# Adaptive-norm two-layer kernel: the first attention stage in another order, with three of its VectorE pieces on GpSimd

## The chip, the core and the metric

The kernel runs on one core of a Trainium2 chip. TensorE (PE) multiplies matrices, VectorE (DVE), ScalarE (ACT) and GpSimd (POOL) work element by element, and SyncE (SP) only issues transfers. Each engine takes its own instructions strictly in the order in which the program lists them; between engines, semaphores hold an instruction until its operands are there. The metric is the time of one execution on the device, in microseconds (us), as the median of the runs.

## What is computed

Two layers, each an attention part and a mixture of experts, each behind a layer norm that a vector `c` modulates. The change touches the attention part of the first layer, for x of 2048 positions by 128 channels:

```python
h = _layernorm(x, axis=-1) * (1 + ca) + sa
z = conv1d(h @ W_in, w_conv, 4 taps, causal, per channel) + b_conv
x_val, x_gate, s_raw = z[..., :D], silu(z[..., D:2*D]), z[..., 2*D:]
time_w = exp(-softplus(slopes) * distance)          # one rate per head, 32 heads
p = exp(clip(score_scale * s_raw, -20.0, 20.0))
phi = x_val * theta                                  # 4 angles per channel
w = softmax(deriv_logits)
poly = w[0] + w[1] * x_val - w[2] * square(x_val)    # the derivative polynomial
p_w = p * time_w                                     # the decayed weights
num_re, num_im, den = cumsum([p_w*poly*cos(phi), p_w*poly*sin(phi), p_w], axis=position)
re, im = num_re / max(den, 1e-4), num_im / max(den, 1e-4)
rsq = rsqrt((sum(re**2) + sum(im**2)) / 32 + 1e-5)   # per head
y = re * rsq * norm_scale @ W_re + im * rsq * norm_scale @ W_im
x = x + ga * (y * x_gate @ W_out)
```

Behind it come the first layer's experts and the whole second layer, which the change leaves as they are.

## The kernel before

**Layout.** Channels lie on the 128 partitions, positions along the free axis, cut into four chunks of 512 (`NC`, `CW`). One instruction over a chunk works on 128x512 elements; one over the four angles of a chunk on 128x2048.

**Start (lines 1651 to 1703).** SP issues the small vectors, both layers' modulation matrices `wmod`, the four pieces of x and the weights. DVE spreads `silu(c)`, PE multiplies it with both `wmod` matrices, DVE turns the results into `modc` and `gar` for both layers, multiplies input and convolution weights into `wfold` (three groups: values, gates, scores), and then does the first layer norm of the four pieces. PE turns each piece (`norm`, line 849), ACT writes it as `hT` (line 1384).

**Projections (line 868).** `values0`, `gates0` and `scores0` of a chunk are four matmuls each, one per tap. PE does values of chunk 0, then the scores of all four chunks, then gates of chunk 0; the others follow inside the loop.

**Weights and angles.** DVE scales and clips a chunk's scores (lines 1814, 1815), ACT takes the exponential (line 1446), and DVE multiplies by the decay table `tw` (line 1819), all four chunks before the loop. `front(c)` on DVE makes the four angles and reduces them to a turn (lines 1719, 1721, 1722); `trig(c)` on ACT takes |x|, cosine and sine (lines 1406 to 1409). `weights(c)` on DVE does the polynomial (1730, 1734), its product with the weights (1735) and the running sum of the denominator (1732).

**The loop over chunks.** `back(c)` on DVE multiplies cosines and sines with the weights (lines 1744, 1745) and makes eight running sums (`TENSOR_TENSOR_SCAN`, line 1752). PE multiplies each sum into `y` as it comes (line 903), ACT squares them (1418), PE adds the squares (909). `mean_square(c)` on DVE floors and squares the denominator (1757, 1758) and adds it (1760), ACT takes the root (1423), `gated(c)` on DVE inverts it (1766), multiplies by the gate and by `y` (1768, 1770), PE multiplies by `W_out` (921), `residual(c)` adds x (1774). DVE's order in round c is `back(c)`, `mean_square(c-1)`, `front(c+1)`, `weights(c+1)`, `gated(c-1)`. PE's in round c is values and gates of chunk c+1, `out0(c-2)`, then the products of chunk c.

**Behind the loop.** The second layer norm (lines 1651 to 1664 again), for which PE first does twenty matmuls with the identity whose result nobody reads (`spare`, line 838), then the router and the experts. GpSimd does almost nothing in this stage.

## Time and profile before

| | us |
|---|---|
| median of 3 runs | 1192.84 |
| lowest and highest | 1191.51, 1195.95 |
| the profiled execution | 1191.35 |
| its span | 1189.6 |
| first attention stage and second norm, in the span | from 0 to about 192 |

The profile holds one execution. DVE is busy for 77% of the span, PE for 91%, ACT for 62%, GpSimd for 21%. A timeline row gives the start and the length in us, the engine, the line, the operation, its output and inputs, the number of instructions and, in brackets, how long the engine sat idle before and which instruction ended that. Rows that hold several instructions give their length together. One matmul of the program on 32-bit numbers is two records of PE, so a projection of four matmuls is eight.

### The profile page before, as it was taken

The numbers are of one execution on the slowest core, as the hardware profiler recorded it, in microseconds if no ns is written. First come the engines' busy times: TensorE is split into PE (matmuls) and PEld (weight loads), VectorE is DVE, ScalarE is ACT, GpSimd is POOL, SyncE is SP. The second block draws the span as 40 slices with busy tenths as digits, with TensorE's granted clock in tenths as the row PEclk, the third lists the DMA queues.
The fourth block names the chain that finished last, engine by engine and source line by source line (L and its number), as shares of the span: only waits on it lengthen the run. The fifth ranks groups of instructions, "written<-read, shape, count | busy, mean of one in ns | idle before, by whom it ended". The sixth has DMA issues, their size and how long they took to land.

```text
span 1189.6 us, 18272 instructions
## 1 busy us (share of the span) xinstructions
PE 1079.5 (91%) x5695; PEld 600.4 (50%) x5711; DVE 916.6 (77%) x1791; ACT 740.3 (62%) x1088; POOL 247.7 (21%) x287
## 2 busy tenths in 40 slices
PE   3898668999999988989999999999979999999998
PEld 2333236477777743322222222222335888888886
DVE  5589998455555485899999999988637888888885
ACT  1645426588888723455667676778765666666664
POOL 0000001289988914431111100111120000000000
PEclk9899879999999999899999999999998999999999
DMA  6000001599898352430000000000000410111001
GB/s 178 1 0 1 1 0 49 110 219 203 195 206 181 71 140 53 66 96 2 2 1 2 2 1 2 1 2 2 1 2 3 160 56 29 40 62 62 0 1 36
DMA packets 40206, 66.58 MB, mean 56 GB/s; under 512 B 14778, under 2 KB 31322, under 8 KB 34778
## 3 DMA queue, kind: packets, MB, share of 16 engines
q1 hardware_dynamic: 40130, 65.56, 22.8%
q8 instruction: 48, 0.79, 0.3%
q14 instruction: 28, 0.23, 0.1%
HBM read 62.30 MB, written 3.11 MB: 55 GB/s over the span
## 4 chain that ended last, share of the span: by engine, by line
PE 61%; DVE 26%; ACT 6%; issue 4%; POOL 1%; DMA 0%; SPq 0%; POOLq 0%; DVEq 0%; ACTq 0%
PE ps L1015 10%; PE ps L1016 10%; PE ps L1017 10%; PE ps L1242 9%; DVE arena_b L2008 8%; PE ps L1178 7%; DVE arena_b L1752 3%; PE ps L1225 3%; PE ps L836 3%; PE ps L1191 2%; POOL parts L775 1%; DVE arena_b L1933 1%; ACT arena_b L1565 1%; PE ps L868 1%; DVE arena_b L2015 1%
## 5 line engine op out<-in xcount | busy, mean ns | idle before, releaser
L1565 ACT ACTIVATE arena_b<-ps 128x1024 f32<-128x1024 f32 (+3 forms) x320 | 272.9, 894 | 134.6 <-PE ps L1225 133.1
L1015 PE MATMUL ps<-parts 128*128 128x512 f32 x640 | 252.5, 394 | 10.2 <-POOL parts L775 7.7
L1017 PE MATMUL ps<-parts 128*128 128x512 f32 x640 | 249.3, 390 | 0.0
L1016 PE MATMUL ps<-parts 128*128 128x512 f32 x640 | 249.3, 390 | 0.0
L2008 DVE TENSOR_REDUCE arena_b<-ps 128x1 f32<-128x512 f32 x384 | 237.9, 682 | 7.0 <-PE ps L1178 5.7
L1178 PE MATMUL ps<-arena_a 48*128 48x512 bf16 (+6 forms) x820 | 180.4, 309 | 17.8 <-DVE arena_b L2008 9.0
L775 POOL TENSOR_TENSOR parts<-arena_b,parts 128x512 fp32r<-128x512 f32 x128 | 166.6, 1313 | 61.4 <-ACT parts L1498 56.8
L1178 PEld LDWEIGHTS ps<-arena_a 48*128 48x128 bf16 (+1 forms) x832 | 60.3, 94 | 204.8 <-DVE arena_b L2008 132.7
L1242 PE MATMUL ps<-arena_b 128*32 128x512 f32 (+3 forms) x1280 | 151.1, 544 | 1.6 <-ACT arena_b L1565 0.8
L1933 DVE SCALAR_TENSOR_TENSOR arena_b<-ps,arena_a 128x512 f32<-128x512 f32 x128 | 87.0, 688 | 79.8 <-PE ps L1017 79.8
L1015 PEld LDWEIGHTS ps<-parts 128*128 128x128 f32 x640 | 120.1, 188 | 48.0 <-POOL parts L775 19.7
L1017 PEld LDWEIGHTS ps<-parts 128*128 128x128 f32 x640 | 120.1, 188 | 25.2
L1016 PEld LDWEIGHTS ps<-parts 128*128 128x128 f32 x640 | 120.2, 188 | 23.7
L1225 PE MATMUL ps<-arena_a 50*128 50x512 bf16 (+3 forms) x640 | 126.4, 351 | 6.0 <-ACT arena_b L1565 4.8
L2115 DVE TENSOR_TENSOR arena_b<-ps,arena_b 128x512 f32<-128x512 f32 x128 | 88.2, 689 | 52.6 <-PE ps L1017 46.8
L1592 ACT ACTIVATE arena_b<-ps 128x512 f32<-128x512 f32 x128 | 76.6, 599 | 82.9 <-PE ps L1017 82.6
L819 POOL TENSOR_SCALAR_AFFINE_SELECT arena_b<-arena_b 128x256 f32<-128x256 f32 x128 | 52.1, 408 | 365.2 <-ACT arena_b L1565 364.1
L1497 ACT ACTIVATE arena_b<-arena_b 128x512 f32<-128x512 f32 x128 | 80.3, 628 | 36.5 <-DVE arena_b L1933 35.4
L2120 DVE TENSOR_TENSOR parts<-arena_b,parts 128x512 fp32r<-128x512 f32 x128 | 87.2, 681 | 0.1
L1596 ACT ACTIVATE parts<-arena_b 128x512 fp32r<-128x512 f32 x128 | 79.8, 624 | 0.4 <-DVE arena_b L2115 0.4
L1498 ACT ACTIVATE parts<-arena_b 128x512 fp32r<-128x512 f32 x128 | 78.9, 616 | 0.0
L2010 DVE TENSOR_REDUCE arena_b<-ps 128x4 f32<-128x512 f32 x64 | 43.0, 690 | 19.5 <-PE ps L1191 19.0
(276 smaller groups left out, 1133.8 us busy)
## 6 DMA issues: line engine op xcount, KB each, us to landing
arena_a<-root_weights SPq DMA_DIRECT2D x60, 512.0 KB, 6.4
arena_b<-expert_weights SPq DMA_DIRECT2D x7, 1024.0 KB, 6.2
arena_a<-q_parts SPq DMA_DIRECT2D x36, 64.0 KB
wslot<-in_L_ffn_up_w SPq DMA_DIRECT2D x8, 256.0 KB, 6.7
wslot<-in_L_ffn_down_w SPq DMA_DIRECT2D x8, 256.0 KB, 7.0
wslot<-in_L_ffn_w_gate SPq DMA_DIRECT2D x8, 256.0 KB, 2.7
wslot<-in_L_ffn_w_up SPq DMA_DIRECT2D x8, 256.0 KB, 3.0
wslot<-in_L_ffn_w_down SPq DMA_DIRECT2D x8, 256.0 KB, 3.6
```

What stands on the lines that cost most here:

```text
L775: g.tensor_tensor(hid0[:, k % NBUF, 1, :], sq0[:, k % NBUF, :], hid0[:, k % NBUF, 0, :].bitcast(F32), ALU.subtract).then_inc(moe_lo, 1)
L1015: mm(bank, w(0), x(0), start=start, stop=False)
L1016: mm(bank, w(0), x(1), start=False, stop=False)
L1017: return mm(bank, w(1), x(0), start=False, stop=stop)
L1178: return mm(b[:, at_:at_ + kw], qst[r, tq // TPC, g, i // 2, tq % TPC * P:(tq % TPC + 1) * P], kst[r, i % 2, g, k0:k0 + kw], start=True, s ...
L1225: last = mm(ps[:, 2 + 2 * pair + i, off:CW], kst[r, i, g, j * P:(j + 1) * P], qst[r, c, g, pair, off:CW], start=True, stop=True)
L1242: last = mm(ps[32 * i:32 * i + 32, 6, off:CW], vaug[:, j, g, :], probs[:, s % 2, i, off:CW], start=(j == 0), stop=(j == TPC * c + TPC - 1) ...
L1565: a(probs[:, s % 2, 2 * pair:2 * pair + 2, off:CW], ps[:, 2 + 2 * pair:4 + 2 * pair, off:CW], ACT.Exp, scale=scale).then_inc(p2_exp, 1)
L1933: v.scalar_tensor_tensor(prod0[:, k % NBUF, :], ps[:, k % 4, :], 0.0, cbw[:, pair % NCBUF, chunk(c)], ALU.max, ALU.mult).then_inc(moe_prod, 1)
L2008: v.tensor_reduce(m8[:, t % TPC, 4 + u:5 + u], b, AX_X, ALU.max).then_inc(slot_read, 1)
L2115: v.tensor_tensor(prod1[:, k % NBUF, :], ps[:, 2 + k % 2, :], silg[:, k % 2, :], ALU.mult)\
L2120: v.tensor_tensor(hid1[:, k % NBUF, 1, :], prod1[:, k % NBUF, :], hid1[:, k % NBUF, 0, :].bitcast(F32), ALU.subtract).then_inc(ffn_lo, 1)
```

## The change

SP: the second layer's `wmod` is loaded behind the convolution weights, and the decay table counts on `ld_b`, so that weights no longer wait for it. PE: only layer 0's modulation comes first; ten spare matmuls; turning, values and scores are interleaved; layer 1's modulation goes to bank 6; six projections instead of three stand ahead of the router's transpose, and `values0` runs two chunks ahead. ACT: `trig(0)` and `trig(1)` both come ahead of the loop, the exponentials of the scores of chunks 1 to 3 inside round 0. DVE: the statistics of x start before the modulation, `front` runs two chunks ahead (its first two ahead of the loop), scores 2 and 3 are scaled between the running sums of chunk 0, layer 1's modulation and two of the four pieces' statistics for the second norm stand ahead of the last `mean_square`, and `weights(c)` is the running sum alone. GpSimd: `polynomial(c)` and `floor(c)`, seven instructions for each chunk. `floor` multiplies by the root of 1e-5 before it squares, where DVE scaled the square. Nothing else of the arithmetic changes.

```diff
             nc.gpsimd.memset(hT[:, 0:PAD], 0.0).then_inc(pad_zero, 1)
...
+            def polynomial(c):
+
+                x, t, part = xv[:, c % 2, :], tmp[:, 0, :], pw[:, chunk(c)]
+                pool.wait_ge(xv_ready, c + 1)
+                if c == 0:
+                    pool.wait_ge(slope_ready, 2)
+                    pool.wait_ge(tw_ready, 1)
+                pool.wait_ge(zs_exp, c + 1)
+                nc.gpsimd.tensor_tensor(part, part, tw[:, chunk(c)], ALU.mult).then_inc(pw_ready, 1)
+                chain(nc.gpsimd.tensor_scalar(t, x, dw[:, 2:3], dw[:, 1:2], ALU.mult, ALU.add))
+                chain(nc.gpsimd.tensor_tensor(t, t, x, ALU.mult))
+                chain(nc.gpsimd.tensor_scalar(t, t, dw[:, 0:1], None, ALU.add))
+                if c >= 2:
+                    pool.wait_ge(num_ready, 2 * M0 * (c - 2) + 1)
+                nc.gpsimd.tensor_tensor(pw_poly[:, c % 2, :], t, part, ALU.mult).then_inc(pw_ready, 1)
+
+            def floor(c):
+
+                t = tmp[:, 1 + c % 2, :]
+                pool.wait_ge(xv_used, c + 1)
+                if c >= 2:
+                    pool.wait_ge(q_ready, c - 1)
+                chain(nc.gpsimd.tensor_scalar(t, den[:, chunk(c)], 1e-4, EPS ** 0.5, ALU.max, ALU.mult))
+                nc.gpsimd.tensor_tensor(t, t, t, ALU.mult).then_inc(pw_ready, 1)
+
+            for c in range(NC):
+                polynomial(c)
+                floor(c)
...
             for c in range(NC):
                 if c == 1:
+                    pe.wait_ge(rw_ready, 2)
+                if c + 1 < NC:
+                    gates0(c + 1)
+                if c + 2 < NC:
+                    values0(c + 2)
+                if c == 0:
+                    scores0(3)
                     pe.wait_ge(rw_ready, 1)
...
+            trig(0)
+            trig(1)
+            gates(1)
             for c in range(NC):
-                if c + 1 < NC:
-                    values(c + 1)
-                    gates(c + 1)
-                squares(c)
+                if c + 2 < NC:
+                    values(c + 2)
+                if 1 <= c < NC - 1:
+                    trig(c + 1)
+                squares(c, 0)
+                if c == 0:
+                    for k in range(1, NC):
+                        decays(k)
+                squares(c, 1)
                 if c >= 1:
                     root(c - 1)
-                if c + 1 < NC:
-                    trig(c + 1)
+                if c + 2 < NC:
+                    gates(c + 2)
...
             def weights(c):
 
-                b = c % 2
-                x = xv[:, b, :]
-                if c == 0:
-                    dve.wait_ge(pw_ready, NC)
-                step(v.tensor_scalar(tmp[:, 0, :], x, dw[:, 2:3], dw[:, 1:2], ALU.mult, ALU.add))
+                dve.wait_ge(pw_ready, 3 * c + 1)
                 prev = den[:, c * CW - 1:c * CW] if c else 0.0
-                step(v.tensor_tensor_scan(den[:, chunk(c)], ones_b, pw[:, chunk(c)], prev, ALU.mult, ALU.add))
-                settle()
-                chain(v.tensor_tensor(tmp[:, 0, :], tmp[:, 0, :], x, ALU.mult))
-                chain(v.scalar_tensor_tensor(pw_poly[:, b, :], tmp[:, 0, :], dw[:, 0:1], pw[:, chunk(c)],
-                                             ALU.add, ALU.mult))
-                v.tensor_copy(tiny[:, 46:47], tiny[:, 45:46]).then_inc(xv_used, 1)
+                v.tensor_tensor_scan(den[:, chunk(c)], ones_b, pw[:, chunk(c)], prev, ALU.mult, ALU.add)\
+                    .then_inc(xv_used, 1)
 
             def back(c):
 
                 b = c % 2
                 dve.wait_ge(trig_ready, c + 1)
+                dve.wait_ge(pw_ready, 3 * c + 2)
...
+                    if c == 0 and n in (1, 3):
+                        decay_scores(2 + n // 2)
 
             def mean_square(c):
 
-                chain(v.tensor_scalar(tmp[:, 1, :], den[:, chunk(c)], 1e-4, None, ALU.max))
-                chain(v.scalar_tensor_tensor(tmp[:, 1, :], tmp[:, 1, :], EPS, tmp[:, 1, :], ALU.mult, ALU.mult))
+                dve.wait_ge(pw_ready, 3 * c + 3)
                 dve.wait_ge(ss_mm, c + 1)
...
             for c in range(NC):
                 back(c)
                 if c >= 1:
                     mean_square(c - 1)
+                if c + 2 < NC:
+                    front(c + 2)
                 if c + 1 < NC:
-                    front(c + 1)
                     weights(c + 1)
+                if c == 0:
+                    dve.wait_ge(ld_b, 64)
+                    v.tensor_tensor(wo0[:, :], wo0[:, :], gar[:, 0, :], ALU.mult).then_inc(bd_ready, 1)
                 if c >= 1:
                     gated(c - 1)
                 if c >= 3:
                     residual(c - 3, 2 + (c - 3) % 2, o0_mm, x1_ready)
+            residual(1, 3, o0_mm, x1_ready)
+            dve.wait_ge(rw_ready, 1)
+            modulation(1, modc[:, 1, 0:5], gar[:, 1, :])
+            stats1(0)
+            stats1(1)
             mean_square(NC - 1)
-            residual(NC - 3, 2 + (NC - 3) % 2, o0_mm, x1_ready)
             gated(NC - 1)
```

On DVE, the middle of a round in the kernel before, from the floored denominator of the chunk behind to the inversion of its root (`arena_a`, `arena_b` hold all stage-1 tiles, `tiny` the per-channel scalars, `ones_w` a column of ones, `ps` is PSUM):

```order
L1757 TENSOR_SCALAR arena_a<-arena_a 128x512
L1758 SCALAR_TENSOR_TENSOR arena_a<-arena_a 128x512
L1760 SCALAR_TENSOR_TENSOR arena_a<-ps,arena_a 128x512
L1719 TENSOR_SCALAR arena_a<-arena_a,tiny 128x512 x4
L1721 TENSOR_SCALAR arena_b<-arena_a 128x2048
L1722 TENSOR_TENSOR arena_a<-arena_b,arena_a 128x2048
L1730 TENSOR_SCALAR arena_a<-arena_a,tiny 128x512
L1732 SCALAR_TENSOR_TENSOR arena_a<-ones_w,arena_a 128x512
L1734 TENSOR_TENSOR arena_a<-arena_a 128x512
L1735 SCALAR_TENSOR_TENSOR arena_a<-arena_a,tiny 128x512
L1737 COPY tiny<-tiny 128x1
L1766 RECIPROCAL arena_b<-arena_a 128x512
```

And the same stretch of the changed kernel in the round that still has a `front` in it; in the last two rounds the rows 1846 to 1849 are missing, and in the very last 1855 too:

```order
L1881 SCALAR_TENSOR_TENSOR arena_a<-ps,arena_a 128x512
L1846 TENSOR_SCALAR arena_a<-arena_a,tiny 128x512 x4
L1848 TENSOR_SCALAR arena_b<-arena_a 128x2048
L1849 TENSOR_TENSOR arena_a<-arena_b,arena_a 128x2048
L1855 SCALAR_TENSOR_TENSOR arena_a<-ones_w,arena_a 128x512
L1887 RECIPROCAL arena_b<-arena_a 128x512
```

Six instructions of a round have left DVE. On GpSimd these seven stand once for each chunk, behind the zero padding:

```order
L764 TENSOR_TENSOR arena_a<-arena_a 128x512
L765 TENSOR_SCALAR arena_a<-arena_a,tiny 128x512
L766 TENSOR_TENSOR arena_a<-arena_a 128x512
L767 TENSOR_SCALAR arena_a<-arena_a,tiny 128x512
L770 TENSOR_TENSOR arena_a<-arena_a 128x512
L778 TENSOR_SCALAR arena_a<-arena_a 128x512
L779 TENSOR_TENSOR arena_a<-arena_a 128x512
```

That is four with two tensors read and three with one. On PE, the beginning of the program before, up to the router's transpose (line 927), behind which ACT's copy of it is waited for:

```order
L857 MATMUL ps<-arena_a 128x128
L859 MATMUL ps<-tiny,arena_a 128x1 x5
L857 MATMUL ps<-arena_a 128x128
L859 MATMUL ps<-tiny,arena_a 128x1 x5
L849 MATMUL ps<-ident,xn 128x128 x16
L868 MATMUL ps<-hT,arena_a 128x512 x24
L927 MATMUL ps<-ident,rwn 128x64
```

And now, where 889 and 891 are the modulation, 871 the spare matmuls, 901 the turned pieces of x, 906 the projections and 983 the router's transpose:

```order
L889 MATMUL ps<-arena_a 128x128
L891 MATMUL ps<-tiny,arena_a 128x1 x5
L871 MATMUL ps<-ident 128x128 x10
L901 MATMUL ps<-ident,xn 128x128 x4
L889 MATMUL ps<-arena_a 128x128
L891 MATMUL ps<-tiny,arena_a 128x1 x5
L901 MATMUL ps<-ident,xn 128x128 x4
L906 MATMUL ps<-hT,arena_a 128x512 x8
L901 MATMUL ps<-ident,xn 128x128 x8
L906 MATMUL ps<-hT,arena_a 128x512 x16
L983 MATMUL ps<-ident,rwn 128x64
```

The first two projections (values and scores of chunk 0) have moved ahead of the last two pieces of x, and ACT's trigonometry of chunk 0 stands behind its copy of the router's transpose.

## Rows read from the trace of the kernel before

**Rows 1.** Busy time by stretch: start:end, length, PE, PEld, DVE, ACT, POOL; PEclk, DMA share, GB/s.

```profile
63.00:85.00 22.00, 19.77 (x43) 8.41 (x42) 21.79 (x22) 8.05 (x6) 0.00 (x0) 0.92 0.00 0
```

**Rows 2.** Timeline of DVE in the attention stage.

```profile
52.93 0.81 DVE L1814 TENSOR_SCALAR arena_a<-ps,tiny 128x512 f32<-128x512 f32 x1 [5.45 <-PE ps L868]
...
63.37 2.28 DVE L1744 TENSOR_TENSOR arena_b<-arena_b,arena_a 128x2048 f32<-128x2048 f32 x1
...
76.84 1.65 DVE L1719 TENSOR_SCALAR arena_a<-arena_a,tiny 128x512 f32<-128x512 f32 x4
...
81.99 0.54 DVE L1730 TENSOR_SCALAR arena_a<-arena_a,tiny 128x512 f32<-128x512 f32 x1
82.45 1.28 DVE L1732 TENSOR_TENSOR_SCAN arena_a<-ones_w,arena_a 128x512 f32<-128x512 f32 x1
...
88.12 2.29 DVE L1744 TENSOR_TENSOR arena_b<-arena_b,arena_a 128x2048 f32<-128x2048 f32 x1 [2.69 <-ACT tiny L1411]
...
102.08 0.40 DVE L1757 TENSOR_SCALAR arena_a<-arena_a 128x512 f32<-128x512 f32 x1
...
103.25 0.69 DVE L1760 SCALAR_TENSOR_TENSOR arena_a<-ps,arena_a 128x512 f32<-128x512 f32 x1
...
164.00 3.35 DVE L1766 RECIPROCAL arena_b<-arena_a 128x512 f32<-128x512 f32 x1 [2.15 <-ACT arena_a L1423]
...
176.00 0.69 DVE L1770 TENSOR_TENSOR xn<-ps,arena_b 128x512 f32<-128x512 f32 x1
```

**Rows 3.** Timeline of DVE at the start of the program.

```profile
12.17 0.16 DVE L1675 COPY modc<-ps 128x5 f32<-128x5 f32 x1 [5.43 <-PE ps L859]
...
15.50 1.29 DVE L1699 TENSOR_TENSOR arena_a<-arena_a 128x512 f32<-128x512 f32 x2
...
17.51 0.86 DVE L1651 BATCH_NORM_STATS2 stats<-xt 128x6 f32<-128x128 f32 x4
...
18.90 0.87 DVE L1651 BATCH_NORM_STATS2 stats<-xt 128x6 f32<-128x128 f32 x4
...
20.82 1.12 DVE L1664 TENSOR_SCALAR xn<-xt,mv,rstd 128x128 f32<-128x128 f32 x4
```

**Rows 4.** DMA issues of x: line, count, KB of each, median us to landing.

```profile
xt<-in_L_attn_x SPq DMA_DIRECT2D x4, 256.0 KB, 5.1
```

**Rows 5.** Timeline of PE: projections, then spare matmuls behind the loop.

```profile
29.39 11.54 PE L868 MATMUL ps<-hT,arena_a 128*128 128x512 f32 x24
46.45 13.31 PE L868 MATMUL ps<-hT,arena_a 128*128 128x512 f32 x24 [5.51 <-DVE arena_a L1815]
...
59.90 7.14 PE L868 MATMUL ps<-hT,arena_a 128*128 128x512 f32 x16
...
178.61 6.12 PE L838 MATMUL ps<-ident 128*128 128x128 f32 x40
```

**Rows 6.** Timeline of ACT: |x| of the angles of chunk 1.

```profile
82.11 1.91 ACT L1406 ACTIVATE arena_b<-arena_a 128x2048 f32<-128x2048 f32 x1 [3.24 <-DVE arena_a L1722]
```

**Rows 7.** GpSimd's groups by shape in the whole program: count, busy us, mean ns.

```profile
L775 POOL TENSOR_TENSOR parts<-arena_b,parts 128x512 fp32r<-128x512 f32 x128 | 166.6, 1313 | 61.4 <-ACT parts L1498 56.8 <-issue 0.6
...
L796 POOL CAST arena_a<-arena_b 128x512 bf16<-128x512 f32 x6 | 3.7, 612 | 0.1
L798 POOL TENSOR_TENSOR arena_b<-arena_b,arena_a 128x512 f32<-128x512 f32 x3 | 3.5, 1156 | 0.1
```

**Rows 8.** Line 1852 of DVE over the program: ns min/median/max, first and last start.

```profile
L1852 DVE TENSOR_TENSOR parts<-wslot,parts x16: 685/1432/1437, 192.7 to 380.5; 128x512 fp32r<-128x512 f32 x16
```

**Rows 9.** Timelines of GpSimd and DVE in the first layer's experts.

```profile
262.50 1.29 POOL L775 TENSOR_TENSOR parts<-arena_b,parts 128x512 fp32r<-128x512 f32 x1 [0.77 <-ACT parts L1498]
264.06 1.44 POOL L775 TENSOR_TENSOR parts<-arena_b,parts 128x512 fp32r<-128x512 f32 x1 [0.27 <-ACT parts L1498]
...
262.91 1.43 DVE L1852 TENSOR_TENSOR parts<-wslot,parts 128x512 fp32r<-128x512 f32 x1 [1.14 <-ACT parts L1468]
264.26 1.27 DVE L1933 SCALAR_TENSOR_TENSOR arena_b<-ps,arena_a 128x512 f32<-128x512 f32 x2
```

More of the change, by code:

```diff
@@ new lines, in stats0, with scaled0 @@
+                settle()
+                for t in tiles(c):
+                    step(v.bn_aggr(mv[:, t, :], stats[:, t, :]))
+                settle()
+                m = mv[:, TPC * c:TPC * c + TPC, 1]
+                v.tensor_scalar(m, m, EPS, None, ALU.add).then_inc(ln_var, 1)
+            def scaled0(c):
+                ts = slice(TPC * c, TPC * c + TPC)
+                dve.wait_ge(ln_sd, c + 1)
+                chain(v.reciprocal(rstd[:, ts], sd[:, ts]))
+                for t in tiles(c):
+                    last = v.tensor_scalar(xn[:, t, :], xt[:, t, :], mv[:, t, 0:1], rstd[:, t:t + 1],
+                                           ALU.subtract, ALU.mult)
+                last.then_inc(ln_xn, 1)
@@ new lines, in _ @@
+            ones_b = ones_w[:, :].broadcast_to([P, CW])
+            dve.wait_ge(silu_c, 1)
+            for l in range(2):
+                v.tensor_copy(scb[:, l, :], tiny[:, 2 + l:3 + l].broadcast_to([P, P])).then_inc(scb_ready, 1)
+            step(v.memset(ones_w[:, :], 1.0))
+            chain(v.memset(nsc, HALF_PI))
+            stats0(0)
+            stats0(1)
+            scaled0(0)
+            dve.wait_ge(mod_mm, 1)
+            modulation(0, ps[:, 3, 0:5], ps[:, 2, 0:P])
+            dve.wait_ge(ld_a, 32)
@@ L1808, in _, with stats1 @@
             last.then_inc(bd_ready, 1)
[L1809 to L1819 removed]
             weights(0)
+            def stats1(c):
+                dve.wait_ge(x1_ready, c + 1)
+                for t in tiles(c):
+                    step(v.bn_stats(stats[:, t, :], xt[:, t, :]))
             for c in range(NC):
```

218 lines of the change are left out of this document (129 added, 89 removed).

## The prediction, made before the changed kernel ran

> **What bounds the kernel now.** I first read the busy time by stretch: in the attention stage, the two rounds from 63 to 85 us keep DVE busy for 21.8 of 22.0 us, while ACT has 8.0, GpSimd 0 and PE 19.8 (a PE whose matmuls mostly wait for DVE's sums looks busy) [rows 1]. Then DVE's own timeline. Each round is two multiplications of 2048 columns, eight running sums and the small work around them; from the first weighted multiplication (start 63.37) to the end of the last gated product (176.69) are 113.3 us, and I found only two waits of more than 1 us in it, 2.69 for the trigonometry of chunk 1 and 2.15 for a root [rows 2]. So DVE is the path there, and each us taken from it counts, unless something else comes late. Before 63.37 the path goes by turns over DVE, PE and ACT: DVE for instance stands 5.45 us for a projection at 47.5 [rows 2]. Everything behind the last gated product is a fixed chain (output product, spare matmuls, second norm, router, experts, layer 1) that I take to shift as a whole. The sum therefore has three terms: when the first weighted multiplication starts, how long DVE takes from there to the last gated product, and what GpSimd's work costs DVE.
>
> **Term 1, the start.** On DVE: a piece's statistics take 18.90 - 17.51 = 1.4 us, normalising it 1.3 with its reciprocal, the modulation of both layers 15.50 - 12.17 = 3.3, so one layer 1.65, and a folded weight group 0.65 [rows 3]. x lands about 5.1 us after its issue [rows 4]; the first issue is now at about 2.2 (one 0.46 us issue earlier than at 2.69), so at 7.3. Then 2 x 1.4 + 1.3 + 1.65 + 0.65 + 1.4 + 1.3 = 9.1 until piece 1 is normalised, at 16.4, and 1.1 for PE to turn it: the first projection can start at 17.5, against 29.39 before [rows 5]. But six projections (48 records) now stand ahead of the router's transpose and of ACT's `trig(0)`. At full clock a record takes 7.14 / 16 = 0.446, so 21.4 us; two pieces turned, the transpose and one wait for `hT` add about 2.4; ACT's copy 0.25. `trig(0)` takes 88.12 - 82.11 = 6.0 [rows 6]. That gives 17.5 + 21.4 + 2.4 + 0.25 + 6.0 = 47.5. PE comes from idling, and there its clock is at the lower of its two levels: the 24 records behind an idle time of 5.51 took 13.31, not 10.7 [rows 5]. If the first two projections run at half speed, 7 us more: 54.5. The new spare matmuls speak for less, so I take 3 of the 7: 50.6. Term 1 is 50.6 - 63.4 = -12.8 us, with bounds -15.9 and -8.9.
>
> GpSimd's first polynomial waits for the decay table's exponential and chunk 0's, both of which stand on ACT two steps ahead of the transpose's copy, so before 44.6 in this count; its five instructions (5.2 us, priced below) end before 49.8. That hides under `trig(0)` (50.6) with about 1 us to spare, and is the next thing to come late.
>
> **Term 2, DVE from there.** Removed: `front(1)` moves ahead of the start, 81.99 - 76.84 = 5.2. `weights` of chunks 1 to 3 keep only the running sum: from 81.99 to 85.43 (where the wait of 2.69 begins) are 3.4 us, the sum alone takes 1.2 in a row, so 3 x 2.2 = 6.6. `mean_square` loses two instructions, 103.25 - 102.08 = 1.17, four times: 4.7. Waits removed: 2.69, since `trig(1)` is done a round earlier, and 2.15 [rows 2]. Sum -21.3. Added: scaling and clipping two chunks of scores between running sums, 2 x (0.8 + 0.4) = 2.4; `wo0` 0.2; modulation of layer 1, 1.7, and two pieces' statistics, 2 x 0.9, moved ahead of the last `mean_square`. And new waits for the root: before, `front` and `weights` (8.5 us) lay between a `mean_square` and its `gated`. Now in round 2 only a sum of 1.2 does, in round 3 nothing. The root path is as long as the wait before shows with nothing in between: about 3.3 with its table load (2.15 plus what DVE did meanwhile, here 1.2), so new waits of about 2, 2 and 0.7, together 4.7. Sum +10.8. Term 2 is -10.5 us, so without any cost of GpSimd the stage ends 23.3 us earlier. Behind it two pieces' statistics have gone from the second norm, worth nothing: PE still does its spare matmuls, 6.1 us [rows 5], before it looks at the first piece.
>
> **Term 3, what GpSimd takes back.** It gets 28 instructions, 16 with two tensors read and 12 with one. The nearest rows: 1.16 to 1.31 for 512 columns with two inputs, 0.61 with one (a cast) [rows 7]. I take 1.29 and 0.65 (with 1.0 as the upper bound, since scale and offset come from a column): 28.4 us in four rounds of about 24, so GpSimd is not short of time itself. But the trace shows that it doesn't run beside DVE for free. Line 1852 on DVE reads two tensors of SBUF; alone it takes 0.69 us, and in the experts' part, where GpSimd multiplies, 1.43 [rows 8]. One of them, seen closely: GpSimd runs from 262.50 to 263.79, DVE's starts at 262.91 and ends at 264.34, which is its 0.69 counted from 263.65. It stood still until GpSimd was nearly done. GpSimd's next, started at 264.06, took 1.44 instead of 1.29, and DVE's line 1933, with one input from PSUM, isn't touched (1.27 for two) [rows 9]. So two-input DVE work from SBUF and GpSimd's work exclude each other, and each full collision costs DVE about 1.29 - 0.25 = 1.05 us, or 0.4 with a short GpSimd instruction. Nearly all of a round is such work on DVE: the multiplications and, if they behave alike, the running sums, which read a tensor and a column of ones. What isn't is the reciprocal (3.35) and what reads PSUM.
>
> How many collide: `polynomial(0)` (5) comes while DVE has small work or waits for `trig(0)`; `floor(2)`, `floor(3)` and about one more (5) fall beside reciprocals and waits for the root. The other 18, some 10 long and 8 short: 10 x 1.05 + 8 x 0.4 = 13.7, of which about 1 goes into the waits for the root. Term 3 is +12.6 us; if all 28 collide 21.6, if only the multiplications exclude GpSimd about 6, if nothing does, 0.
>
> The Trainium skill (SBUF — State Buffer, 🔬 SBUF: two separate sides) calls the second SBUF port pair of VectorE and GpSimd an exclusive lock, held for the whole instruction by a VectorE instruction with two SBUF inputs or in a two-port mode. By that rule the running sums take part too, which no row here can show, since GpSimd stands still in the stage before; the sum above goes by it, and without it term 3 would be the 6.
>
> **Sum.** -12.8 - 10.5 + 12.6 = -10.7 us. The profiled execution took 1191.35, so 1180.6; it lies 1.5 under the median of its runs, 1192.84, and against the median the forecast is 1182.1. A measurement of this kernel can tell about 0.5%, 6 us, from no change.
>
> **The rivals.**
> A, the forecast: multiplications and running sums both exclude GpSimd. 1182.1; with the bounds of term 1 and 1.0 for the short GpSimd instructions from 1176 to 1189.5. If GpSimd has to wait for a pause of DVE instead of taking turns, fewer of its instructions fall between sums, and it is nearer to 1176.
> B, the running sums leave GpSimd alone: term 3 is 6, 1175.5. For it: the sums read a single column as their second tensor. Against: they are two-input instructions like line 1852.
> C, no collision counts: 1192.8 - 23.3 = 1169.5, with a warm PE 1166. Against it stands the median of 1.43 over the sixteen of line 1852.
> D, slower: PE stays at the lower level (1.2 GHz) through all six projections of the start, because its work there comes in pieces with waits for `hT` between. That is 21.4 us more on term 1, less the 3 taken: +18.3, and 1200.4. Each projection at half speed costs 3.5: with four the gain is gone, and only with all six is the kernel slower by over 6. Before, both groups of 24 records lost less than 3 us to it [rows 5].
> E, the two-input work costs GpSimd far more than its rows (its `tensor_scalar` with a column at 2 us): 12 x 1.3 more, half of it beside DVE, 1190 to 1196, no change.
>
> **How the numbers follow.** A 0.55, B 0.15, C 0.12, D 0.08, E 0.10. A lies by more than 6 us below in about five of six cases, E seldom. Faster 0.74, same 0.18, slower 0.08. The predicted time is A's, 1182. The range of 8 in 10 reaches from C's warm end to A's upper bound: 1166 to 1190; D and most of E lie above.
>
> **What would show it.** Term 1: the first multiplication of 2048 columns starts near 50, and the projections from 17.5. Term 2: no wait for the trigonometry of chunk 1, waits for the root in the last three rounds. Term 3: multiplications of 2.28 and sums of 1.26 that take up to 1.1 more where GpSimd runs, and GpSimd instructions far longer than 1.29; sums at 1.26 beside a busy GpSimd mean B, multiplications at 2.28 too mean C. Spacings of 0.86 between PE's records in all the early projections mean D; GpSimd's `tensor_scalar` at over 1.5 in the clear means E. The prediction is wrong as a whole if something behind the last gated product doesn't shift with it.

## The result, and the profile after

The changed kernel takes 1177.44 us (median of 4, 1176.94 to 1177.81) beside 1192.17 of the kernel before in the same session; the ratio is 0.9872 with a 95% interval from 0.9847 to 0.9898. That is 14.7 us faster, where 10.7 were forecast (1182). The profiled execution has a span of 1175.9 us, 13.7 less than before.

DVE's timeline of the changed kernel, the places that answer to [rows 2] (start us, us, engine, line, operation, tiles and shapes, count, idle time before and what ended it):

```profile
47.61 2.74 DVE L1864 TENSOR_TENSOR arena_b<-arena_b,arena_a 128x2048 f32<-128x2048 f32 x1 [1.17 <-POOL arena_a L770]
50.27 3.12 DVE L1865 TENSOR_TENSOR arena_a<-arena_a 128x2048 f32<-128x2048 f32 x1
...
80.39 6.76 DVE L1872 TENSOR_TENSOR_SCAN arena_b<-ones_w,arena_b 128x512 f32<-128x512 f32 x4
...
127.16 3.35 DVE L1887 RECIPROCAL arena_b<-arena_a 128x512 f32<-128x512 f32 x1 [2.14 <-ACT arena_a L1489]
...
136.40 4.81 DVE L1872 TENSOR_TENSOR_SCAN arena_b<-ones_w,arena_b 128x512 f32<-128x512 f32 x4
...
148.41 3.35 DVE L1887 RECIPROCAL arena_b<-arena_a 128x512 f32<-128x512 f32 x1 [1.91 <-ACT arena_a L1489]
...
158.74 3.35 DVE L1887 RECIPROCAL arena_b<-arena_a 128x512 f32<-128x512 f32 x1 [0.69 <-ACT arena_a L1489]
...
162.85 0.69 DVE L1891 TENSOR_TENSOR xn<-ps,arena_b 128x512 f32<-128x512 f32 x1
```

The first weighted multiplication starts at 47.61 instead of 63.37, so 15.8 us are won ahead of it ("the start"). The rest up to the last gated product is called the stage below. It goes from there to the end of the last gated product (163.54), 115.9 us, against 113.3 before: 2.6 lost. Together 13.15, and the span shows 13.7. The whole gain lies in the start, and the stage itself, which the move of work to GpSimd was to shorten, is longer than before.

PE's start, which answers to [rows 5]: the first 16 projection records come at 0.44 us each, and there is one wait of 1.10.

```profile
16.00 7.03 PE L906 MATMUL ps<-hT,arena_a 128*128 128x512 f32 x16
22.88 1.03 PE L901 MATMUL ps<-ident,xn 128*128 128x128 f32 x8
25.01 13.98 PE L906 MATMUL ps<-hT,arena_a 128*128 128x512 f32 x32 [1.10 <-ACT arena_a L1465]
38.92 0.27 PE L983 MATMUL ps<-ident,rwn 64*128 64x64 f32 x1
```

The exclusion that [rows 8, 9] showed in the experts is now in the stage. GpSimd's and DVE's timelines around 86 us, on one clock:

```profile
86.16 2.05 POOL L766 TENSOR_TENSOR arena_a<-arena_a 128x512 f32<-128x512 f32 x1
87.06 2.23 DVE L1872 TENSOR_TENSOR_SCAN arena_b<-ones_w,arena_b,arena_a 128x512 f32<-128x512 f32 x1
```

GpSimd's multiplication ends at 88.21; the running sum, issued at 87.06, ends at 89.29, which is 1.08 behind that: it stood still until GpSimd was done. So a running sum takes part too (rival B falls). What DVE lost in all is read from its groups between 40 and 165 us in the changed kernel, and then from the same groups between 40 and 155 us of a version in which GpSimd does nothing in the stage (e7 below; its line 1843 is 1846 here). Columns: busy us, mean ns of one.

```profile
L1872 DVE TENSOR_TENSOR_SCAN arena_b<-ones_w,arena_b 128x512 f32<-128x512 f32 x16 | 22.4, 1456 | 0.1
L1872 DVE TENSOR_TENSOR_SCAN arena_b<-ones_w,arena_b,arena_a 128x512 f32<-128x512 f32 x12 | 16.8, 1456 | 0.0
L1865 DVE TENSOR_TENSOR arena_a<-arena_a 128x2048 f32<-128x2048 f32 x4 | 11.5, 2863 | 0.0
L1872 DVE TENSOR_TENSOR_SCAN arena_b<-ones_w,arena_a 128x512 f32<-128x512 f32 x4 | 5.6, 1458 | 0.0
L1846 DVE TENSOR_SCALAR arena_a<-arena_a,tiny 128x512 f32<-128x512 f32 x8 | 5.0, 690 | 0.1
```

```profile
L1872 DVE TENSOR_TENSOR_SCAN arena_b<-ones_w,arena_b 128x512 f32<-128x512 f32 x16 | 19.1, 1252 | 0.1
L1872 DVE TENSOR_TENSOR_SCAN arena_b<-ones_w,arena_b,arena_a 128x512 f32<-128x512 f32 x12 | 14.4, 1259 | 0.0
L1865 DVE TENSOR_TENSOR arena_a<-arena_a 128x2048 f32<-128x2048 f32 x4 | 9.1, 2284 | 0.0
L1843 DVE TENSOR_SCALAR arena_a<-arena_a,tiny 128x512 f32<-128x512 f32 x8 | 3.3, 483 | 0.1
L1872 DVE TENSOR_TENSOR_SCAN arena_b<-ones_w,arena_a 128x512 f32<-128x512 f32 x4 | 4.6, 1201 | 0.0
```

The running sums lose 44.8 - 38.1 = 6.7, line 1865 2.4, line 1846 1.7, and four smaller groups 2.5 (1864: 0.5, 1849: 0.9, 1889: 0.9, 1848: 0.2). That is 13.3 us of stretching in the stage. Ahead of it, beside `polynomial(0)`, DVE was stretched too: the eight small multiplications of line 1933 took 3.58 us, 1.71 in e1, where GpSimd does nothing. The 13.3 leave that out.

### The profile page after: what moved, and what is told of

Same layout as the page of the kernel before. It is cut to its first block, busy times and chain, and to the rows that moved or that the text cites. A ratio compares the mean times of both kernels' runs of the same rounds, so it can differ in the third digit from the quotient of the medians.

```text
span 1175.9 us, 18334 instructions
## 1 busy us (share of the span) xinstructions
PE 1081.1 (92%) x5731; PEld 599.3 (51%) x5731; DVE 916.4 (78%) x1763; ACT 735.8 (63%) x1087; POOL 299.4 (25%) x315
## 4 chain that ended last, share of the span: by engine, by line
PE 60%; DVE 25%; ACT 6%; issue 5%; POOL 2%; DMA 0%; SPq 0%; POOLq 0%; DVEq 0%; ACTq 0%
PE ps L1075 10%; PE ps L1077 10%; PE ps L1076 10%; PE ps L1302 9%; DVE arena_b L2136 8%; PE ps L1238 7%; DVE arena_b L1872 3%; PE ps L1285 3%; PE ps L869 2%; POOL parts L810 2%; PE ps L1251 2%; DVE arena_b L2061 1%; ACT arena_b L1654 1%; DVE arena_b L2143 1%; DVE arena_b L1887 1%
## 5 line engine op out<-in xcount | busy, mean ns | idle before, releaser
L1238 PE MATMUL ps<-arena_a 48*128 48x128 bf16 (+5 forms) x832 | 184.9, 310 | 18.3 <-DVE arena_b L2136 9.6
L959 PE MATMUL ps<-arena_b,arena_a 128*128 128x512 f32 x64 | 39.3, 744 | 23.8 <-DVE arena_b L1872 23.6
```

What stands on the lines that cost most here:

```text
L1238: return mm(b[:, at_:at_ + kw], qst[r, tq // TPC, g, i // 2, tq % TPC * P:(tq % TPC + 1) * P], kst[r, i % 2, g, k0:k0 + kw], start=True, s ...
```

## The experiments

All times are medians; "first" is the start of the first weighted multiplication and "last" the end of the last gated product, both in the profiled execution. The before of each session was 1192.6 (e1 to e4), 1196.0 (e6 to e9) and 1190.6 (e5, e10 to e12), so between sessions the ratio with its interval is the surer number. Each trace is of one execution.

| kernel | us | ratio to before | first | last |
|---|---|---|---|---|
| before | 1192.2 | | 63.37 | 176.69 |
| changed | 1177.4 | 0.9872 (0.9847 to 0.9898) | 47.61 | 163.54 |
| e1 new order, work on DVE | 1176.0 | 0.9862 (0.9835 to 0.9889) | 47.33 | 159.44 |
| e2 old order, work on GpSimd | 1196.9 | 1.0039 (1.0021 to 1.0058) | 61.79 | 183.13 |
| e3 no spare matmuls at the start | 1184.3 | 0.9930 (0.9907 to 0.9953) | 49.85 | 165.78 |
| e4 six more on GpSimd | 1183.7 | 0.9918 (0.9892 to 0.9943) | 48.38 | 167.48 |
| e5 floor on DVE | 1180.9 | 0.9918 (0.9901 to 0.9934) | 47.65 | 164.07 |
| e10 other pair of operations | 1178.5 | 0.9905 (0.9883 to 0.9928) | 47.43 | 162.63 |
| e8 start mended | 1174.9 | 0.9829 (0.9792 to 0.9865) | 44.03 | 159.78 |
| e9 e1 with the start mended | 1172.7 | 0.9811 (0.9775 to 0.9846) | 44.87 | 156.97 |
| e6 scalar forms on ACT | 1167.8 | 0.9764 (0.9727 to 0.9802) | 44.21 | 152.51 |
| e7 the same, nothing on GpSimd | 1165.0 | 0.9741 (0.9704 to 0.9778) | 43.61 | 148.79 |
| e11 e7 without the spares | 1169.4 | 0.9822 (0.9806 to 0.9838) | 46.05 | 151.22 |
| e12 e7, ACT's square later | 1165.9 | 0.9783 (0.9760 to 0.9805) | 43.16 | 148.31 |

### e1 and e2: order and move apart

e1 takes the changed kernel and puts the work back on DVE:

```diff
-            for c in range(NC):
-                polynomial(c)          # GpSimd
-                floor(c)
 def weights(c):                        # VectorE
+    step(v.tensor_tensor(pw[:, chunk(c)], pw[:, chunk(c)], tw[:, chunk(c)], ALU.mult))
+    chain(v.tensor_scalar(tmp[:, 0, :], x, dw[:, 2:3], dw[:, 1:2], ALU.mult, ALU.add))
     ... running sum ...
+    chain(v.tensor_tensor(tmp[:, 0, :], tmp[:, 0, :], x, ALU.mult))
+    chain(v.scalar_tensor_tensor(pw_poly[:, b, :], tmp[:, 0, :], dw[:, 0:1], pw[:, chunk(c)], ALU.add, ALU.mult))
 def mean_square(c):
+    chain(v.tensor_scalar(t, den[:, chunk(c)], 1e-4, None, ALU.max))
+    chain(v.scalar_tensor_tensor(t, t, EPS, t, ALU.mult, ALU.mult))
```

> The new order with the decay products, the polynomial and the floor back on VectorE (five instructions for a chunk's weights and two for its floor, as in the kernel before), and nothing of it on GpSimd. Theory A (GpSimd's work costs VectorE about what it takes from it): VectorE gets back 3 x 2.9 + 4.7 = 13.4 us between the first weighted multiplication and the last gated product and loses the stretching of 13 to 16 us that the trace of the changed kernel shows; the first multiplication stays near 47.5. 1174 to 1179 us, no different from the changed kernel, and multiplications at 2.28, running sums at 1.20 throughout. Rival B (the stretching is small change, GpSimd is worth its work): 1183 to 1190.

Measured 1176.0, no different from the changed kernel, and in the trace the stage ends 4.1 us sooner than with GpSimd's help (159.44). The first four sums of its second round, unstretched, and its wait for the root in the fourth:

```profile
77.20 4.81 DVE L1877 TENSOR_TENSOR_SCAN arena_b<-ones_w,arena_b 128x512 f32<-128x512 f32 x4
...
143.12 3.35 DVE L1894 RECIPROCAL arena_b<-arena_a 128x512 f32<-128x512 f32 x1 [0.73 <-ACT arena_a L1486]
```

The account closes. By the spacings of e1's trace the work put back is 12.9 us and not the 13.4 expected: 2.75 for each of the chunks 1 to 3 and 1.16 for each of the four floors. Root waits of 4.74 become 1.42: the wait of 2.14 is filled by the polynomial of chunk 3, and 1.18 of the next by a floor. From the changed kernel's 115.9 take 13.3 of stretching, add 12.9 of work and take 3.3 of waits: 112.2, measured 112.1. So DVE's own work was 12.9 us, and handing it over cost 13.3 of stretching plus 3.3 of waits that nothing fills now.

e2 is the other half: the old order, with the change's `polynomial` and `floor` on GpSimd and its short `weights` and `mean_square` on DVE.

```diff
+            for c in range(NC):            # GpSimd
+                polynomial(c)
+                floor(c)
...
-            for c in range(NC):            # VectorE
-                dve.wait_ge(zs_exp, c + 1)
-                v.tensor_tensor(pw[:, chunk(c)], pw[:, chunk(c)], tw[:, chunk(c)], ALU.mult).then_inc(pw_ready, 1)
```

> The kernel before in its own order, with only the work moved to GpSimd (decay products, polynomial, floor). Theory A: the whole gain lies in the order, so this gains nothing: 1189 to 1195 us, with VectorE's instructions stretched by 12 to 16 us in sum. Rival B (the move is worth its work and the order the rest): 1180 to 1186.

Slower than before, by 4.3 us with an interval that excludes zero, and above both ranges given. DVE is stretched by 12.9 us in the stage and relieved of 11.3, so the stretching alone doesn't do it; new waits do. What was taken from DVE between `front` and `back` had covered the trigonometry of the next chunk, and the floor part of a wait for the root:

```profile
61.79 2.74 DVE L1771 TENSOR_TENSOR arena_b<-arena_b,arena_a 128x2048 f32<-128x2048 f32 x1 [2.75 <-POOL arena_a L770]
...
91.67 2.29 DVE L1771 TENSOR_TENSOR arena_b<-arena_b,arena_a 128x2048 f32<-128x2048 f32 x1 [4.85 <-ACT tiny L1445]
...
171.62 3.35 DVE L1792 RECIPROCAL arena_b<-arena_a 128x512 f32<-128x512 f32 x1 [3.33 <-ACT arena_a L1457]
```

The waits inside the stage grow by 6.2 us: 2.69 become 4.85, two of 1.4 are new, and the root's 2.15 become 3.33. 12.9 - 11.3 + 6.2 = 7.8, and the stage is 8.0 longer than before. So of the two parts the order gives everything (16.6 us alone), and the move alone costs 4. The order is itself a bundle, on SP, PE, ACT and DVE; of its pieces only the spare matmuls were taken out by themselves.

### e3: the spare matmuls

```diff
-            spare(10, 0, ident)
```

> The changed kernel without the ten spare matmuls ahead of the first piece's transposes. Theory (the spare matmuls keep TensorE at the upper level, which is what I had left open in term 1): the first 16 projection records come at spacings near 0.86 instead of 0.44, 3 to 7 us later on TensorE, so the first weighted multiplication starts at 50 to 54 and the time is 1180 to 1184. Rival (the clock is up from the modulation's and the transposes' matmuls anyway, or the projections after the first have enough room): no difference, 1177, first multiplication at 47.6.

The first multiplication starts 2.2 us later, at 49.85. That lies between the theory's 50 to 54 and the rival's 47.6:

```profile
16.35 1.09 PE L901 MATMUL ps<-ident,xn 128*128 128x128 f32 x4
17.23 8.04 PE L906 MATMUL ps<-hT,arena_a 128*128 128x512 f32 x16
```

The projections' records themselves lose 1.0 (8.04 against 7.03): the first two take 1.92 together, where four take 1.88 in the changed kernel, and from there on they come at 0.43. What comes ahead of them loses 1.2. So without the spares PE costs 2.2 here and not the 7 that the prediction put as its bound. The granted clock reads 1.00 from 10 to 26 us in both kernels, so that PE's lower level is the cause is not shown. The median is 6.8 above the changed kernel's, more than the trace shows: the profiled execution took 1179.55 at a mean granted clock of 0.978, and the other four 1183.8 to 1184.7 at 0.972 or 0.973. Several of these kernels show such groups some 5 us apart (e10: twice 1176.1, twice 1181.0, and there the clocks do not tell them apart). I have not found their cause.

### e4: what one GpSimd instruction costs, and its forms in the clear

```diff
+    step(g.memset(tmp[:, 0:2, :], 1.0))
+    step(g.tensor_scalar(t, t, 1e-4, EPS ** 0.5, ALU.max, ALU.mult))
+    step(g.tensor_scalar(t, t, k, k, ALU.mult, ALU.add))     # k: a column
+    step(g.tensor_scalar(t, t, k, None, ALU.add))
+    step(g.tensor_tensor(t, t, t, ALU.mult))
...
+    if c == 0:                                               # behind floor(0)
+        for _ in range(6):
+            chain(nc.gpsimd.tensor_tensor(tmp[:, 0, :], den[:, chunk(0)], den[:, chunk(0)], ALU.mult))
```

> The changed kernel with more work for GpSimd. (1) At the very start, where VectorE stands still, on a scratch tile: a fill, then one each of: maximum and multiplication with two numbers, multiplication and addition with two columns, addition with one column, multiplication of two tensors. This prices the forms in the clear; expected 1.93, 1.0 to 1.2, 1.0 to 1.2, 1.05 to 1.28. (2) Six multiplications of two tensors behind the first floor, all under the running sums of chunk 0, where GpSimd stood still from 51 to 63. If running sums and GpSimd exclude each other, each costs VectorE 0.4 to 1.05 us: 1180 to 1184 us, back of chunk 1 starting 2.4 to 6.3 later than 75.46. If running sums leave GpSimd alone: 1177, and 75.46.

GpSimd's timeline, first the forms at the start and then the six. The form with two columns is cheaper and the one with one column dearer than the 1.0 to 1.2 expected for both:

```profile
1.91 1.92 POOL L786 TENSOR_SCALAR arena_a<-arena_a 128x512 f32<-128x512 f32 x1
3.93 0.77 POOL L787 TENSOR_SCALAR arena_a<-arena_a 128x512 f32<-128x512 f32 x1
4.80 1.58 POOL L788 TENSOR_SCALAR arena_a<-arena_a 128x512 f32<-128x512 f32 x1
6.46 1.04 POOL L789 TENSOR_TENSOR arena_a<-arena_a 128x512 f32<-128x512 f32 x1
...
51.98 11.96 POOL L797 TENSOR_TENSOR arena_a<-arena_a 128x512 f32<-128x512 f32 x6
```

And DVE's beside the six:

```profile
54.20 3.86 DVE L1886 TENSOR_TENSOR_SCAN arena_b<-ones_w,arena_b 128x512 f32<-128x512 f32 x2
57.98 0.78 DVE L1932 TENSOR_SCALAR arena_a<-ps,tiny 128x512 f32<-128x512 f32 x1
...
59.13 3.97 DVE L1886 TENSOR_TENSOR_SCAN arena_b<-ones_w,arena_b 128x512 f32<-128x512 f32 x2
```

The four sums take 3.86 + 3.97 instead of 2.34 + 2.33, and chunk 1's `back` starts 31.0 us behind chunk 0's instead of 27.85: 3.2 us for six, 0.53 each, while GpSimd needs 1.99 for one instead of 1.04. Running sums and GpSimd exclude each other. The price of one is 0.5 here; in the changed kernel it is higher, since the eight sums of round 1 (line 1872 at 80.39 and 87.06) lose 4.4 us to between five and six of GpSimd's instructions, about 0.8 each. Between the sums DVE's scaling of scores, one input from PSUM, keeps its 0.78, beside a GpSimd that is never idle there: it isn't touched.

In the trace the last gated product is 3.9 us later: 3.2 by the six, and 0.8 because everything began later (the convolution weights, for which DVE waits, landed 0.5 later in this execution). The median is 6.3 above the changed kernel's; the rest lies behind the stage.

### e5 and e10: parts of GpSimd's work

e5 takes `floor` alone off GpSimd, the polynomial stays:

```diff
-                floor(c)
 def mean_square(c):
+    chain(v.tensor_scalar(t, den[:, chunk(c)], 1e-4, None, ALU.max))
+    chain(v.scalar_tensor_tensor(t, t, EPS, t, ALU.mult, ALU.mult))
```

> The changed kernel with the floor alone back on VectorE (two instructions of 0.43 and 0.69 a chunk), decay products and polynomial stay on GpSimd. VectorE gets 4.7 us, of which the waits for the root take back some 0.5, and loses what the floors' 8 instructions stretch: of these only those of chunks 0 and 1 fall beside multiplications or running sums (4.08 and 1.64 long instead of 1.93 and 1.04). Theory A (a GpSimd instruction costs VectorE only what overlaps): the floors of chunks 2 and 3 were free, those of 0 and 1 cost about 3, so this is slower by 1 to 2: 1178 to 1180 us. Rival (every part of the move costs more than it takes): 1175 to 1176.

Last gated product 0.5 later; the median of 1180.9 is 3.4 higher and above both ranges given. The account I gave is not what happened. DVE gets 4.7 us of work, and the waits for the root take back 2.4 of it (2.14 and 1.91 become 0.96 and 0.73), not 0.5. The stretching falls by only about 1.8, which is what is left to close the sum: without `floor`, GpSimd starts `polynomial(2)` 10.3 us sooner, straight into DVE's multiplications and sums of round 1 (the eight sums take 7.16 + 7.50, against 6.76 + 7.20). What GpSimd does costs by what it meets, and taking a piece away moves the others.

e10 changes the polynomial's second scaled form, with the same values:

```diff
-chain(nc.gpsimd.tensor_scalar(t, t, dw[:, 0:1], None, ALU.add))
+chain(nc.gpsimd.tensor_scalar(t, t, ones_w[:, 0:1], dw[:, 0:1], ALU.mult, ALU.add))
```

> The changed kernel with the polynomial's last scaled form written otherwise: the addition of one column (1.58 us in the clear by an earlier run) becomes a multiplication by a column of ones and an addition of the column, the form that took 0.77. The same values. Theory (GpSimd's time for one of these depends on the pair of operations): that instruction takes 0.8 to 1.0 instead of 1.82, polynomial(0) ends 0.8 us sooner and with it the first multiplication starts at 46.8, and three later ones stretch less: 1174.5 to 1176.5 us. Rival (the 0.77 came from its place, not its form): no difference, 1177.4.

The instruction falls from 1.82 to 1.13 and from 1.87 to 1.06 in the first two chunks, so its form does set its price. The first multiplication comes only 0.2 sooner and not the 0.8 expected: the polynomial ends 1.1 us earlier, but its last product now meets the running sum ahead of that multiplication, which takes 2.29 instead of 1.21. The medians show no difference (1178.5, where 1174.5 to 1176.5 was expected; the intervals overlap).

### e8 and e9: the start

In the changed kernel `polynomial(0)` waited until 40.03 for the softmax of the derivative weights, which DVE issues behind `front(1)`, and its last instruction ended at 47.51:

```profile
40.03 1.28 POOL L764 TENSOR_TENSOR arena_a<-arena_a 128x512 f32<-128x512 f32 x1 [39.11 <-DVE tiny L1926]
...
45.74 1.77 POOL L770 TENSOR_TENSOR arena_a<-arena_a 128x512 f32<-128x512 f32 x1
```

e8 moves the softmax and the block matrices ahead of `front(0)`, and `trig(0)` ahead of the copy of the router's transpose.

```diff
+            dve.wait_ge(dl_exp, 1)
+            chain(v.reciprocal(dsum, dsum))
...
+            chain(v.tensor_tensor(wrows, wrows, nscale[:, :, :].unsqueeze(3).broadcast_to([P, 2, M0, H0]), ALU.mult))
...
             front(0)
...
             front(1)
-            dve.wait_ge(dl_exp, 1)
-            chain(v.reciprocal(dsum, dsum))
...
             decay_scores(1)
-            chain(v.tensor_tensor(wrows, wrows, nscale[:, :, :].unsqueeze(3).broadcast_to([P, 2, M0, H0]), ALU.mult))
...
 # ScalarE
+            trig(0)
             act.wait_ge(rw_tr, 1)
             a(rwT[:, :], ps[:, 7, 0:E0], ACT.Copy).then_inc(rw_ready, 1)
-            trig(0)
             trig(1)
```

> The changed kernel with three steps ahead of the first weighted multiplication moved: the softmax of the derivative weights (on VectorE) and the building of the block matrices go from behind front(1) to the gap ahead of front(0), where VectorE stands for the first projection, and ScalarE takes trig(0) ahead of the copy of the router's transpose. Theory: polynomial(0) was late by 1.2 us because its weights stood behind front(1), and trig(0) because it stood behind the router. Now trig(0) runs from 36.5 to 42.4, GpSimd's polynomial(0) from about 33.5 under front(1), which it stretches by about 3. The first multiplication starts at 44.5 to 45.5 instead of 47.6: 1174 to 1176 us. Rival (what bounds the start is something else, the projections for instance): 47 and 1177.

e9 is the same edit made in e1.

> The same three steps moved in the kernel with the new order and all of the work on VectorE (order only). VectorE then has front(1), the scores' scaling and chunk 0's five instructions between the second values and the first multiplication: start at 45.2 instead of 47.3. Theory: 1173 to 1175 us. Rival (nothing behind keeps what is gained at the start): 1176.

Both hold, and the start comes 0.5 and 0.3 us sooner than was expected at least: first at 44.03 (3.6 sooner) and 44.87 (2.5 sooner), and the last gated product follows by 3.8 and 2.5. By the medians 2.6 and 3.3, from two sessions; the intervals of the ratios still overlap with those of the kernels without the edit. In e8 GpSimd's polynomial now runs under `front(1)`, whose four short forms take 3.69 instead of 1.67.

### e6 and e7: another split of the work

The polynomial `dw0 + dw1 x + dw2 x^2` with its square completed is one square and one scaling with offset, and the floor a ramp and a square: both are activations. Both versions also have the mended start of e8. e6 leaves GpSimd 8 multiplications, e7 gives these to DVE too.

```diff
+def square_of_polynomial(c):                      # ScalarE
+    step(a(t, xv[:, c % 2, :], ACT.Square, bias=tiny[:, 48:49]))
+    settle()
+    a(t, t, ACT.Identity, bias=tiny[:, 49:50], scale=dw[:, 2:3]).then_inc(ap_ready, 1)
+def floor(c):                                     # ScalarE
+    step(a(t, den[:, chunk(c)], ACT.Relu, bias=tiny[:, 50:51]))
+    settle()
+    a(t, t, ACT.Square, bias=tiny[:, 51:52], scale=EPS ** 0.5).then_inc(ap_ready, 1)
 # e6 on GpSimd, e7 on VectorE:
+tensor_tensor(pw[:, chunk(c)], pw[:, chunk(c)], tw[:, chunk(c)], ALU.mult)
+tensor_tensor(pw_poly[:, c % 2, :], pw_poly[:, c % 2, :], pw[:, chunk(c)], ALU.mult)
```

> As the first of these, and the work split anew: ScalarE works out the polynomial as a square and one scaling with offset (the same polynomial with its square completed) and the floor as two activations, GpSimd keeps only two multiplications for each chunk, 8 instructions instead of 28. Theory A (each GpSimd instruction costs VectorE up to 1.05 us, and ScalarE's cost it nothing): the stretching falls from 14 to 3 to 6 us, the first multiplication starts near 43.5, and the last gated product ends near 151 to 153 instead of 163.5: 1166 to 1170 us. Rival (ScalarE's added 16 instructions, about 10 us, come late for the roots or the squares): waits of over 2 us for the root or the floor, 1172 to 1177.

> As the one before, with the remaining two multiplications of each chunk on VectorE, so that GpSimd does nothing in the stage. VectorE gets 2 x 0.69 a chunk and loses no time by stretching. Theory A (a multiplication handed to GpSimd costs VectorE 0.4 to 1.05, about as much as the 0.69 that it takes): within 2 us of the one before, 1166 to 1170 us, and every multiplication at 2.28 and every running sum near 1.20. Rival (what is stretched lies beside waits, so that GpSimd is worth it): 3 us or more slower than the one before.

e6 is as fast as expected, 1167.8, and e7 at 1165.0 a little faster than its range of 1166 to 1170; they are the best of the study, and both intervals lie below the changed kernel's. Between the two the intervals overlap, but the traces tell them apart by 3.7 us, where I had expected at most 2. 0.6 of it lies ahead of the stage. Five of GpSimd's eight instructions met `front(2)` and one met `front(3)`; DVE's timeline of e6, then of e7:

```profile
60.24 5.47 DVE L1855 TENSOR_SCALAR arena_a<-arena_a,tiny 128x512 f32<-128x512 f32 x4
65.75 2.17 DVE L1857 TENSOR_SCALAR arena_b<-arena_a 128x2048 f32<-128x2048 f32 x1
```

```profile
59.64 1.68 DVE L1843 TENSOR_SCALAR arena_a<-arena_a,tiny 128x512 f32<-128x512 f32 x4
61.35 1.23 DVE L1845 TENSOR_SCALAR arena_b<-arena_a 128x2048 f32<-128x2048 f32 x1
```

Four instructions of 0.43 became four of 1.37, each held up by one of GpSimd's: 0.95 for a multiplication that DVE does itself in 0.69. In the stage the six cost DVE 5.8 us of stretching where doing the work itself takes 4.0, and a wait for a root that this work fills in e7 is 1.3 longer: 3.1, as measured. What ScalarE took over costs it 0.7 to 0.8 for an activation; it costs DVE no stretching, but a wait of 0.79 for `trig(0)`, behind which e12 goes. Its timeline of e7:

```profile
26.78 0.71 ACT L1477 ACTIVATE arena_a<-arena_a,tiny 128x512 f32<-128x512 f32 x1
27.53 0.82 ACT L1479 ACTIVATE arena_a<-arena_a,tiny 128x512 f32<-128x512 f32 x1
```

### e11 and e12: two touches on e7

```diff
-            spare(10, 0, ident)                     # e11
...
-            square_of_polynomial(1)                 # e12
             gates(0)
...
             trig(0)
+            square_of_polynomial(1)                 # e12
```

> The version with nothing on GpSimd (polynomial and floor on ScalarE, products on VectorE), without the ten spare matmuls at the start. In the changed kernel their absence moved the first multiplication by 2.2 us in the trace, yet the median by 6.8. Theory (what the spares give is the 2.2 us of the start): 1167 to 1168 us, first multiplication at 45.8. Rival (the absence costs more further behind, through TensorE's granted clock): 1170 to 1172.

> The same version with its spares, and ScalarE's square and scaling for chunk 1 behind trig(0) instead of ahead of it: VectorE waited 0.79 for trig(0) there. Theory: first multiplication at 42.8 instead of 43.6, 1164 us. Rival: no difference.

e11: first at 46.05, 2.4 later, as in e3; the profiled span is 2.5 longer and the median 4.5, at 1169.4 between the theory's 1168 and the rival's 1170. The two medians are from two sessions. The spares are worth at least what the start shows; whether the other 2 are theirs stays open. e12 removes the wait of 0.79 and starts 0.45 sooner (0.8 expected); the medians can't tell it from e7.

## Why the prediction was right, and where it was off

**What bounds the kernel.** Right: the stage follows DVE, and what is behind the last gated product shifts with it (13.15 us there, 13.7 in the span). In e1 it did not; see the end.

**Term 1, the start: -12.8 forecast, -15.8 measured.** This is the term that was mis-sized, and nearly all of the error. Three parts of it: the first projection started at 16.0, not 17.5, since x landed sooner (its statistics start at 6.11, not 7.3); the 3 us that I took for a PE at its lower clock level were not there, as the records at 0.44 show; and what lies between the first projection and the end of `trig(0)` was 0.7 shorter than counted. With the spares gone (e3) the start is 2.2 later, so the 7 that I read from [rows 5] as the upper end was no measure for this start. By these three `trig(0)` was done at 45.32, 5.3 ahead of the forecast 50.6, and 2.3 of that were lost again. DVE itself was ready only at 46.44, and `polynomial(0)` came late by another 1.2: I had it end at 49.8 with 1 us to spare, because it would wait for ACT's exponentials. It waited for DVE, behind `front(1)`, a step that the prediction did not list among what stands ahead of it, and then took 7.5 instead of 5.2. That it was "the next thing to come late" was right, and e8 shows the cure.

**Term 2, DVE's own work: -10.5 forecast.** The stage without its stretching is 115.9 - 13.3 = 102.6, against 113.3: -10.7. The three new root waits of "about 2, 2 and 0.7" are 2.14, 1.91 and 0.69.

**Term 3, GpSimd's price: +12.6 forecast, +13.3 measured.** Right in its sum, and in the point on which rivals A and B differ, but its parts were partly wrong and made up for each other. A collision with running sums costs 0.5 (e4) to 0.8 and not 1.05. That the sum came out is in part luck. On the other side GpSimd's scaled forms take 0.77 to 1.92 in the clear, where I took 0.65, and `front`'s one-input forms from SBUF, which I had left out, are stretched as well: four take 3.39 instead of 1.65.

```profile
65.96 3.39 DVE L1846 TENSOR_SCALAR arena_a<-arena_a,tiny 128x512 f32<-128x512 f32 x4
```

The Trainium skill (SBUF — State Buffer, 🔬 SBUF: two separate sides) names this too: beside two-input instructions, `tensor_scalar` in a two-port mode takes the shared pair. I had cited the rule for two inputs and for two-port modes and then counted only the first. The trace agrees, as both kinds are stretched, though no row shows which mode an instruction runs in; and it agrees with the exemption: one input from PSUM stays at 0.78 (e4).

**The rivals.** B falls (sums stretched), C falls (13.3 us), D falls (no record near 0.86), E came true in its cause and by its own sign, with forms at 1.58 and 1.92, but not in its price. The time alone could not have told this: 1177.4 is nearer to B's 1175.5 than to A's 1182.1. Nor does A's lower end of 1176 follow from the bounds: with term 1 at -15.9 they give 1192.8 - 15.9 - 10.5 + 12.6 = 1179.0, and the measured time is under that. What the sum of terms hid is that terms 2 and 3 cancel: by the prediction's own numbers the move of work gives 6.6 + 4.7 = 11.3 and costs 12.6, so the change was worth its order alone. That reading was there to be made before the run; e1 and e2 bear it out.

## What to carry to other kernels

Before VectorE's work goes to GpSimd, price it by what it will run beside: next to VectorE work from SBUF (running sums, multiplications, short scaled forms) it costs 0.5 to 1.0 us of VectorE's time for each 512 columns, about what VectorE needs itself (0.69 for a multiplication). Free are only pieces that fall beside PSUM reads (0.78 in e4), waits, or reciprocals: `floor(2)` ran its 1.93 + 1.04 beside one, which kept its 3.33. Ask ScalarE first, if it has time: here scale, offset, square and ramp cost it 0.7 to 0.8 us each and VectorE one wait of 0.79. And look at what the removed work was covering (e2): a shorter engine on the path shows the next wait.
